# Eight-slot maximum in a segment softmax: three halving passes against one strided reduction (Trainium2, one core)

## The reference

```
w_m = (efeat @ W_msg + b_msg).reshape(E, in_f, -1)
w_a = (efeat @ W_attn + b_attn).reshape(E, in_f, -1)
h_src = feat[src][:, :, None]
e1 = w_m * h_src
e2 = w_a * h_src
seg_max = jax.ops.segment_max(e2, dst, num_segments=N)
ex = jnp.exp(e2 - seg_max[dst])
denom = jax.ops.segment_sum(ex, dst, num_segments=N)
attn = ex / denom[dst]
ft = jax.ops.segment_sum(e1 * attn, dst, num_segments=N)
return ft.sum(axis=1)
```

## Time and profile before

| | |
|---|---|
| median of 3 runs | 2643.93 us (2642.5 to 2649.0) |
| profiled execution | 2653.84 us, span 2652.0 us |
| PE busy | 1889.6 us, 71% |
| DVE busy | 2005.1 us, 76% |
| ACT busy | 1480.2 us, 56% |
| POOL busy | 1323.4 us, 50% |
| mean granted TensorE clock | 0.892 of full speed |

### The profile page before, as it was taken

The page is one execution under the profiler, slowest core; times in us unless marked ns, Lnnn a source line. Parts: engine busy times, 40 slices in busy tenths (PEclk is TensorE's granted clock), DMA queues, the critical chain, the costliest instruction groups (busy, mean ns, idle before and its releaser), DMA issues.

```text
span 2652.0 us, 38454 instructions
## 1 busy us (share of the span) xinstructions
PE 1889.6 (71%) x5872; PEld 711.2 (27%) x5873; DVE 2005.1 (76%) x3290; ACT 1480.2 (56%) x5083; POOL 1323.4 (50%) x1556
## 2 busy tenths in 40 slices
PE   2446666477982587787777777778787888788872
PEld 1111111132341133233333333323333333333330
DVE  5778999652011588888888888888888898888883
ACT  5134544110001577677777767677777777677762
POOL 2200000315556565656666656656666666566653
PEclk9788988788975699999999999999999898999986
DMA  2010000000001000000000000000000000000010
GB/s 31 16 27 0 0 0 0 2 10 18 11 12 15 9 10 10 9 10 9 10 9 10 10 9 10 9 10 9 10 9 10 9 10 9 10 9 10 9 9 9
DMA packets 87258, 26.30 MB, mean 10 GB/s; under 512 B 63118, under 2 KB 84224, under 8 KB 87104
## 3 DMA queue, kind: packets, MB, share of 16 engines
q0 software_dynamic: 37824, 18.62, 5.9%
q1 hardware_dynamic: 49327, 6.96, 1.7%
q10 hardware_dynamic: 80, 0.43, 0.1%
HBM read 23.30 MB, written 2.51 MB: 10 GB/s over the span
## 4 chain that ended last, share of the span: by engine, by line
issue 30%; DVE 23%; PE 23%; DVEq 16%; ACT 4%; POOL 2%; DMA 1%; another core or an unknown queue 0%; ACTq 0%; PEldq 0%; POOLq 0%; PEld 0%
PE pair L808 9%; DVE eo L1434 6%; DVE hot L1162 4%; DVEq L1453 3%; ACT eo L997 3%; PE pw L699 3%; PE pw L795 3%; DVE eo L1477 2%; DVE eo L1468 2%; PE pw L696 2%; PE pw L695 2%; DVE top L1449 2%; DVE top L1454 2%; DVE bank L1462 1%; PE pair L804 1%
## 5 line engine op out<-in xcount | busy, mean ns | idle before, releaser
L617 POOL DMA_INDIRECT nbr<-table,rec x960 | 995.2, 1037 | 547.6 <-ACT eo L997 285.1
L808 PE MATMUL pair<-eo,ident 128*128 128x512 f32 x1856 | 886.3, 622 | 10.4 <-issue 7.7
L997 ACT ACTIVATE eo<-pw,nbr 128x32 f32<-128x32 f32 x3776 | 705.5, 370 | 78.7 <-issue 63.2
L1434 DVE TENSOR_TENSOR eo<-pw,nbr 128x1024 f32 (+1 forms) x357 | 423.3, 1218 | 160.8 <-issue 87.3
L795 PE MATMUL pw<-wk,termsT 100*128 100x512 bf16 x954 | 314.7, 416 | 257.9 <-issue 182.4
L808 PEld LDWEIGHTS pair<-eo,ident 128*128 128x128 f32 x1856 | 364.7, 200 | 488.7 <-issue 472.6
L1162 DVE TENSOR_SCALAR hot<-iota_key,near_key 128x500 bf16<-128x500 f16 x974 | 273.5, 345 | 67.7 <-issue 38.9
L986 ACT ACTIVATE eo<-eo 128x2048 f32<-128x2048 f32 x117 | 223.5, 1910 | 105.3 <-DVE eo L1468 75.1
L1468 DVE TENSOR_TENSOR eo<-eo,bank (+1 forms) x117 | 267.6, 2287 | 10.8
L1477 DVE TENSOR_TENSOR eo<-eo x232 | 272.6, 1216 | 3.7 <-issue 3.7
L660 PE MATMUL bank<-hot 128*128 128x500 bf16 x488 | 150.1, 424 | 149.3 <-DVE hot L1162 101.8
(11 more groups left out here) (244 smaller groups left out, 1822.3 us busy)
## 6 DMA issues: line engine op xcount, KB each, us to landing
nbr<-table,rec POOLq DMA_INDIRECT x960
rec<-unit_recs SPq DMA_DIRECT2D x122, 8.0 KB
attr<-in_edge_attr_dram,rec POOLq DMA_INDIRECT x120
unit_recs<-place SPq DMA_DIRECT2D x27, 64.0 KB
shared<-key_row SPq DMA_DIRECT2D x1, 1600.0 KB, 6.5
counts<-in_dst_dram SPq DMA_DIRECT2D x1, 448.0 KB
counts<-in_src_dram SPq DMA_DIRECT2D x1, 448.0 KB
place<-in_src_dram,at_i POOLq DMA_INDIRECT x26, 2.6
```

Source lines behind the costliest of these rows:

```text
L617: pool.indirect_dma_start(nbr[:, b, j * FEAT:(j + 1) * FEAT], None, table, bass.IndirectOffsetOnAxis(ap=rec[:, b, j:j + 1], axis=0)).then_ ...
L808: mm = pe.matmul(total, ident[:], eo[:, ring, j * 2 * CH:(j + 1) * 2 * CH], start=False, stop=(j == SLOT - 1), skip_group_check=True)
L997: done = act.activation(eo[:, ring, lo:lo + wide], pw[:, j - 4, c * wide:(c + 1) * wide], ACT.Copy, scale=nbr[:, held, j * FEAT + c:j * FE ...
L1434: dve.tensor_tensor(eo[:, bass.ds(ring, 1), k * 4 * CH:(k + 1) * 4 * CH] .rearrange("p r (c f) -> p (r c) f", f=2 * FEAT), pw[:, 2 * (k % ...
```

## The change

The three halving maxima become one tensor_reduce over the slots: its input is read with the slot as the innermost index, so that eight numbers that lie 512 fp32 apart make one of 256 results. `top4` and `top2` go, and with them two drains. The finishing steps of a tile move: `inverse` stays behind the maximum, `quotient` goes behind L1464, `outcome` behind L1468. `levels` gets a floor of two units for each tile, and the unit records room for it.

```diff
-UMAX = E // SLOT + NB // SLOT + NT + 4 * SLOT
+UMAX = E // SLOT + NB // SLOT + 2 * NT + 4 * SLOT
...
-        top4 = sb("top4", [P, 4 * CH])
-        top2 = sb("top2", [P, 2 * CH])
...
-                dve.tensor_scalar(lev_f[:], deg_max[0:1, :], float(SLOT - 1), float(SLOT), ALU.add, ALU.max)
+                dve.tensor_scalar(lev_f[:], deg_max[0:1, :], float(SLOT - 1), float(2 * SLOT), ALU.add, ALU.max)
...
-                dve.tensor_tensor(wide(top4[:]), attention(ring, 0, 4), attention(ring, 4, 8), ALU.max
+                dve.tensor_reduce(top1[:].rearrange("p (c o) -> p c o", o=FEAT),
+                                  attention(ring).rearrange("p (s c) o -> p c o s", s=SLOT), AX_X, ALU.max
                                   ).then_inc(s_attr_free, 1)
                 if ended:
                     inverse(*ended)
-                dve.drain()
-                dve.tensor_tensor(top2[:], top4[:, 0:2 * CH], top4[:, 2 * CH:4 * CH], ALU.max)
-                if ended:
-                    quotient(*ended)
-                dve.drain()
-                dve.tensor_tensor(top1[:], top2[:, 0:CH], top2[:, CH:2 * CH], ALU.max)
-                if ended:
-                    outcome(*ended)
                 dve.drain()
                 dve.scalar_tensor_tensor(out=after, in0=before, ...)
                 dve.scalar_tensor_tensor(out=mdiff[:], in0=before, ...).then_inc(s_md, 1)
+                if ended:
+                    quotient(*ended)
                 dve.drain()
                 here = attention(ring).rearrange("p (s c) o -> p s c o", s=SLOT)
                 dve.tensor_tensor(here, here, ..., ALU.subtract).then_inc(s_d, 1)
+                if ended:
+                    outcome(*ended)
...
-                n = dve.snap(units, min_val=1, max_val=E)
+                n = dve.snap(units, min_val=2, max_val=E)
```

## The result

The changed kernel takes 2711.9 us (median of 4 runs, 2708.0 to 2715.7) against 2643.2 us before: ratio 1.024, 95% interval 1.021 to 1.028. That is slower by 69 us of medians; the forecast was slower by 42.

A forecast was written before the change was run, and what follows sets the result against it. DVE's list was taken to bound some units, the circle of PE and ACT the others. Terms of 23.5, 17.4, 0 and 1.0 us gave +42 on the 2643.9 us median, so 2686 us (+1.6%), range 2633 to 2775.

The forecast's parts named there:

- Two circles: DVE sets the pace in 24 of 116 units; in 92 it waits for PE's product 2, 119.3 us in all.
- R: Length of the new strided reduce on DVE: 3.5 us, at 1.63 ns per number as in L1504; upper end 4.7.
- Rival 1: The reduce takes one number per step: 2.29 us, d = -0.2, total 2620 to 2639 us; chance 0.15.
- rival 2: The large step costs more than in L1504: reduce 4.4 to 4.7 us, total 2767 to 2796 us; chance 0.22.
- The gap in front of L1462: Behind the maximum on DVE, a drain and address work for L1462 stay: 0.36 us kept.
- d: Added length of DVE's list per unit: 3.86 us against 2.86, so +1.0 us, carried as 0.98.
- What reaches the end: Waits before the third L1434 hide part of the longer maximum; +42 us shows, 115 if nothing were hidden.
- The walk: Unit-by-unit sum over DVE's 116 units, d less each wait before L1434: 23.5, 17.4 and 0 us, plus 1.0 before the loop.
- rival 3: PE and ACT keep their pace and DVE catches up in its waits: +3 to +17 us, 2647 to 2661; chance 0.13.
- Costs set to nothing: Late s_attr_free on POOL, the two-unit floor and UMAX with freed buffers were to add no time.
- Consequences named ahead: Idle time before L1434 from 119.6 to about 46 us, DVE busy about +136 us, ACT's waits for L1468 and L1464 longer.

The follow-up runs named there:

- experiments 1 to 6: Variants of the kernel before and the changed kernel on two occasions and chips; the kernel before took 2434.5 us (1 to 4) and 2439.4 us (5 and 6).
- address_early: The kernel before with the two offsets into the running maximum computed ahead of the first maximum: 2437.0 us, ratio 1.0005.
- moved_only: The kernel before with quotient and outcome moved and floor and UMAX changed, the three halving maxima kept: 2437.6 us, ratio 0.999.
- first pair: The kernel before and the changed kernel as first measured, chip not on record: 2643.2 and 2711.9 us, ratio 1.024.
- experiment 7: The kernel before and the changed kernel rerun as they stand on a third occasion: 2752.0 and 2754.2 us, ratio 1.001.
- act_slow_before: The kernel before with a drain and an unread copy of 1024 numbers per partition on ACT ahead of last_pair's activations: 2551.4 us against 2439.4.
- costs: The kernel before with fifteen kinds of single DVE operations ahead of the attention: 2048-number reduces at steps 1 or 2 took 2286 ns, at step 512 3592 ns.
- before_again: The kernel before, nothing changed, run once more for a profile on the third occasion: 2752.0 us.
- after_again: The changed kernel run once more as it stands, against the kernel before at 2439.4 us: 2565.4 us, ratio 1.052.
- the copy on ACT: The same drain and extra ACT copy added to both kernels: changed kernel 2569.3 us against 2551.4 for the kernel before, ratio 1.007.
- experiment 8: Changed kernel reducing five of eight slots: 2731.9 us, ratio 0.992; kernel before without its last halving: 2736.1 us, 0.993.

## Why the prediction was right, and where it was off

**What bounds the kernel.** Two circles, DVE's list and PE with ACT, close to each other: right. That the shares of waits between them are a property of the kernel: wrong. On the occasions of experiments 1 to 6 DVE is the bound in nearly all units (idle 9 to 16 us in front of the scaling operations in address_early and moved_only), in the first pair in part of them, in experiment 7 in few. That the waits are waits for PE's product 2 was right too, though the earlier trace rows gives 67.1 of the 119.6 us to no releaser: nearly all of them end 0.28 or 0.29 us behind PE's last product, as do those of act_slow_before, where the view names PE for every one.

**R.** 3.50 us forecast, 3.64 measured; the nearest row, L1504, and a charge for each number read were the right guides. The charge is 0.64 ns for each (0.66 inside the kernel), and L1504 showed 0.58. Rival 1 (2.29 us) is what steps of 1 or 2 cost, rival 2 (4.4 us or more for the large step or for the results) exists in no pattern that was tried (3811 ns was the longest). The Trainium skill's Advanced Engine Details and Errata, SBUF Cachelines, says that a walk to another 16-byte line with each access is charged; costs agrees on where the charge begins, between 8 and 16 bytes, and adds its size, but two lines visited in turn (L1431, 2329 ns) went free.

**The gap in front of L1462.** 0.36 us carried, 0.38 measured. With R this gives d = 1.17 where 0.98 was summed.

**What reaches the end.** The walk, done again with d = 1.17 on the same profile, gives 54.8 us, and 56 with the maximum ahead of the loop, in place of 42. (In the recorded sum 43 x 0.98 - 24.8 is 17.3 and not 17.4, which changes nothing.) So the term of the sum that was mis-sized is d, 0.98 for 1.17 us, and most of that is the length of the reduce: 14 of the 27 us that were missing. The two walks differ by 59.9 us and the two profiled executions by 58.2 (2712.0 - 2653.8), 2 to 4 us above the 56. The remaining 10 us lie between single executions and medians: the profiled execution of before stood 10 us above its median, that of after did not; why is not known.

**The lateness is carried (rival 3).** I gave it 0.13, and in the first pair it did not happen: 59.9 us against 54.8 by the walk without carrying. But where waits are plentiful it does happen: on before_again the walk gives 29 us and the medians show +2; on act_slow_before it gives 50 and 18 show. Where waits are scarce nothing can be carried and the walk is near: 128 us on address_early, 125.3 measured between its walk and that of after_again (1672.6 - 1547.3). So the walk is no bound: where waits are plentiful it was far too high, in the first pair 2 to 13 us too low (56 against 58.2 to 69), where waits are scarce 3 too high. The prediction's reason against carrying, that a late DVE soon makes ACT late, failed on those two occasions, and that the walk came near in the first pair is in part luck. What holds in all four pairs is the account of DVE's list: the growth of the walk and the waits given up in front of the scaling operations make 125 us (59.9 + 65.3) in the first pair, 133 (125.3 + 7.6) from address_early to after_again, 127 (16.5 + 110.9) with the copy on ACT and 116 (-4.5 + 120.1) in experiment 7, against 1.17 x 116 = 136 that were added. How much of it becomes time and how much comes out of waits is what differs.

**Costs set to nothing.** The late s_attr_free: POOL never waits for it in the changed profile. The moved steps, the floor and UMAX: moved_only, 0.999.

**Consequences named ahead.** Idle time in front of the scaling operations 46 us forecast, 54.3 found; DVE's busy time +136 forecast, +150.4 found (2155.5 - 2005.1); longer waits of ACT, as found.

**What stays open.** Why the same kernel takes 2434 to 2752 us on different occasions. The profiles show where part of it lies: pauses that no semaphore explains, in front of last_pair's activations and, for DVE, in front of the maximum. Nothing was tried that would make or remove them, and chip and time changed together. Why lateness is carried in one pair and not in another is open as well. No version that takes the whole maximum was faster than the kernel before; the two of experiment 8, which leave slots out, were so by 0.7 to 0.8%.

## What to carry to other kernels

Price a strided read by the bytes from one number to the next: 4 and 8 bytes were free here, from 16 bytes on it cost 0.63 to 0.74 ns more for each number, except with two numbers to a result, and in this kernel this outweighs two saved instructions and two drains. Before fusing passes, count elements: halving reads two inputs at once, so 8 to 1 takes 1024 + 512 + 256 = 1792 steps, against 2048 for the reduce. Without the charge the reduce would still come out a little ahead, by its fewer fixed parts and drains: 2.29 us (the time of step 1) against 2.50 (1.22 + 0.69 + 0.42 and two gaps). It is the charge that turns the sign. When two circles are nearly equal, a first estimate of what a longer operation costs is d less the waits of each unit. It came near where waits were few or scattered as in the first pair, and was far too high in the two others (50 us for 18, 29 for 2); and it holds for the occasion whose profile was read, so the waits should be read on more than one chip.

## What the hardware showed that I had not expected

The kernel before took 2434.5, 2439.4, 2643.2 and 2752.0 us (medians) on four occasions, and the change cost, in the order of those where it ran, +126 us (2439.4), +69 us (2643.2) and +2 us (2752.0): the slower the occasion, the cheaper the change. Durations of single operations on DVE and ACT's exponential hardly differ between them (the scaling operations 1215 to 1220 ns, the exponential 1909 to 1910, the large step's reduce 3643 to 3661). PE's do: from 900 to 2350 us one matmul of its sums (L808) takes 604 ns in address_early and 612 in moved_only, 624 in the first profile and 641 in before_again, at a mean granted clock of 0.96, 0.96, 0.94 and 0.92. So PE is slower too on the slow occasions; its share of the difference was not separated. Not all of the difference lies in the loop either: it starts at 835.6 us in address_early and at 893.6 in the first profile. What differs most to the eye are pauses of the engines' own. ACT's timeline in before_again:

```profile
1874.22 0.29 ACT L997 ACTIVATE eo<-pw,nbr 128x32 f32<-128x32 f32 x1 [1.08 <-issue]
1874.93 2.25 ACT L997 ACTIVATE eo<-pw,nbr 128x32 f32<-128x32 f32 x12 [0.42 <-issue]
```

and in moved_only, 32 activations in one piece:

```profile
1819.57 5.80 ACT L997 ACTIVATE eo<-pw,nbr 128x32 f32<-128x32 f32 x32
```

The pause of 0.42 us in before_again falls between two of the 32 activations, which wait for nothing between them. The idle time in front of L997 in the loop is 0 in address_early and moved_only (the occasions of 2434 and 2439 us), 73.7 us in the first profile and 133.1 us in before_again; in front of the first step of the maximum it is 0, 30.9 and 32.8 us.
